# Two reciprocals per attention chunk, written as GpSimd powers with exponent minus one

## What is computed

```
fk = jnp.fft.rfft(k, axis=-1)
fk = fk / (jnp.abs(fk) + EPS)          # EPS = 1e-8
fq = jnp.fft.rfft(q, axis=-1)
fq = fq / (jnp.abs(fq) + EPS)
fv = jnp.fft.rfft(v, axis=-1)
fkv = jnp.cumsum(fk * fv, axis=-2)
values_hat = jnp.fft.irfft(fkv * jnp.conj(fq), n=D, axis=-1)
return x + values_hat
```

## Time and profile before

| | |
|---|---|
| median of three runs | 2069.51 us |
| lowest and highest run | 2063.09 and 2073.0 us |
| span of the profiled execution | 2101.2 us |
| attention stage, about | 750 to 1340 us of the span |
| VectorE busy in that stretch | 483.00 of 590 us |
| TensorE busy in that stretch | 395.29 of 590 us |
| GpSimd busy in that stretch | 175.54 of 590 us |
| ScalarE busy in that stretch | 154.13 of 590 us |

### The profile page before, as it was taken

How to read it: one execution, slowest core, us unless ns; L and a number is a source line. 1 busy time by engine, 2 the same in 40 slices (tenths; PEclk the granted TensorE clock), 3 DMA queues, 4 the chain that set the end, 5 groups by cost and what they waited for, 6 DMA issues and landing times.

```text
span 2101.2 us, 35984 instructions
## 1 busy us (share of the span) xinstructions
PE 1652.2 (79%) x10302; PEld 1458.4 (69%) x10303; DVE 1419.4 (68%) x3362; ACT 656.2 (31%) x1094; POOL 767.4 (37%) x868
## 2 busy tenths in 40 slices
PE   3999999679999647676767775599999967999940
PEld 2788888669999536555555553478888857999940
DVE  4778787535555368979898987377877753555557
ACT  3333333134444223232322231233333313444410
POOL 0454443324444323333333332144444422444420
PEclk9999999889999867776777776599999978999975
DMA  8211111144444311010101000011111114444459
GB/s 275 76 52 41 51 51 44 44 122 131 134 134 129 102 41 41 20 40 20 40 20 40 20 20 0 31 55 50 44 54 47 45 46 122 133 132 136 129 183 349
DMA packets 123782, 170.37 MB, mean 81 GB/s; under 512 B 14881, under 2 KB 105394, under 8 KB 123442
## 3 DMA queue, kind: packets, MB, share of 16 engines
q1 hardware_dynamic: 89938, 91.05, 15.0%
q0 software_dynamic: 25344, 70.29, 9.1%
q10 hardware_dynamic: 8448, 8.39, 1.1%
HBM read 91.03 MB, written 81.89 MB: 82 GB/s over the span
## 4 chain that ended last, share of the span: by engine, by line
PE 58%; DVE 17%; issue 9%; DMA 7%; ACT 3%; POOL 3%; SPq 2%; another core or an unknown queue 0%; DVEq 0%; POOLq 0%; ACTq 0%
PE bank L608 17%; PE bank L610 16%; PE bank L609 15%; PE bank L723 3%; DMA lists<-a_rows,a_slots 3%; POOL lists L405 3%; PE bank L733 2%; DMA f_yf<-results 2%; DVE t_cum L1151 2%; DVE t_rn L1133 2%; DVE a_gate_u L971 1%; PE bank L827 1%; DVE X L1214 1%; PE bank L632 1%; DVE t_pr L1149 1%
## 5 line engine op out<-in xcount | busy, mean ns | idle before, releaser
L416 POOL DMA_INDIRECT results<-b_yb,b_goal x272 | 261.6, 962 | 370.5 <-DVE b_yb L1074 297.8
L405 POOL DMA_INDIRECT lists<-a_rows,a_slots x256 | 259.7, 1014 | 117.5 <-issue 64.5
L1074 DVE COPY b_yb<-bank 128x512 f32<-128x512 f32 x136 | 94.1, 692 | 188.4 <-PE bank L610 180.0
L608 PE MATMUL bank<-t_xah,t_wfh 128*128 128x512 f32 x192 | 114.0, 594 | 111.8 <-DVE t_xal L848 61.7
L608 PE MATMUL bank<-ew_h,b_hth 128*128 x544 | 161.5, 297 | 20.3 <-issue 9.9
L608 PE MATMUL bank<-ew_h,b_xbth 128*128 x544 | 165.3, 304 | 1.0 <-DVE b_xbtl L848 1.0
L608 PE MATMUL bank<-a_sw2h,a_uh 128*128 128x256 f32 x512 | 150.4, 294 | 12.6 <-DVE a_ul L848 7.3
L455 ACT ACTIVATE b_hth<-bank 128x512 fp32r<-128x512 f32 x136 | 81.3, 598 | 246.7 <-PE bank L723 239.5
L609 PE MATMUL bank<-ew_l,b_xbth 128*128 x544 | 152.8, 281 | 0.0
L610 PE MATMUL bank<-ew_h,b_xbtl 128*128 x544 | 152.4, 280 | 0.0
L610 PE MATMUL bank<-ew_h,b_htl 128*128 x544 | 152.3, 280 | 0.0
(11 more groups left out here) (209 smaller groups left out, 5114.0 us busy)
## 6 DMA issues: line engine op xcount, KB each, us to landing
b_xb<-lists SPq DMA_DIRECT2D x272, 132.0 KB
t_yg<-results SPq DMA_DIRECT2D x32, 512.0 KB, 4.7
f_yf<-results SPq DMA_DIRECT2D x32, 512.0 KB, 10.9
X<-in_L_attn_x SPq DMA_DIRECT2D x16, 512.0 KB
out<-X ACTq DMA_DIRECT2D x16, 512.0 KB, 7.1
results<-b_yb,b_goal POOLq DMA_INDIRECT x272
w_raw_ew<-in_L_ffn_ew SPq DMA_DIRECT2D x2, 2048.0 KB, 14.3
lists<-a_rows,a_slots POOLq DMA_INDIRECT x256
```

Source lines behind the costliest of these rows:

```text
L405: pool.indirect_dma_start(out=lists, out_offset=bass.IndirectOffsetOnAxis(ap=slots[:, q, k, j:j + 1], axis=0), in_=rows[:, q, j, :], in_of ...
L416: pool.indirect_dma_start(out=results, out_offset=bass.IndirectOffsetOnAxis(ap=goal[:, slot, blk:blk + 1], axis=0), in_=YB[:, slot, blk, : ...
L608: pe.matmul(o, a("h"), b("h"), start=first, stop=False)
L1074: dve.tensor_copy(YB[:, slot].rearrange("p b d -> p (b d)"), bank[:, 7 - par, :]).then_inc(s_yok, 1)
```

## The change

The two reciprocals leave VectorE. Each becomes a GpSimd `tensor_tensor` with the operation power, whose second operand is the constant -1 of `neg_one`, read 512 times from one element per partition. VectorE keeps the two additions of the epsilon, which now signal `s_keps` and `s_qeps`; the multiplication of `FK` is moved behind the second of them and waits for `s_kinv`. On GpSimd the key power stands ahead of the addition to `X`, the query power behind it, followed by a wait for itself and the multiplication of `FQ`.

```diff
-DVE_A, DVE_T = 84, 57
+DVE_A, DVE_T = 84, 51
...
+            def inverse(i):
+                return pool.tensor_tensor(RN[:, i, :], RN[:, i, :], neg_one[:, 0:1].to_broadcast([P, N]), ALU.pow)
+
             def attention(s, par, half):
...
                 if nxt:
                     rstd_of(1 - par, s + (CH + 2))
+                if now:
+                    pool.wait_ge(s_keps, s + 1)
+                    inverse(0).then_inc(s_kinv, 1)
+                if nxt:
                     pool.wait_ge(s_txn, s + 2)
                     xc = X[:, bass.ds((s + 1) * J, J), :]
                     pool.tensor_tensor(xc, xc, XN[:], ALU.add).then_inc(s_add, 1)
                 if now:
-                    pool.wait_ge(s_qinv, s + 1)
+                    pool.wait_ge(s_qeps, s + 1)
+                    ch.link(inverse(1))
+                    ch.settle()
                     pool.tensor_tensor(FQ[:], FQ[:], RN[:, 1:2, :].to_broadcast([P, 2, N]), ALU.mult).then_inc(s_qn, 1)
...
-            run_steps(pool, attention, -1, 2, CH - 2, CH, 2, ch, 6)
+            run_steps(pool, attention, -1, 2, CH - 2, CH, 2, ch, 8)
...
                     dve.wait_ge(s_kroot, s + 1)
-                    ch.link(dve.tensor_scalar(RN[:, 0, :], RN[:, 0, :], FFT_EPS, None, ALU.add))
-                    ch.settle()
-                    ch.link(dve.reciprocal(RN[:, 0, :], RN[:, 0, :]))
-                    ch.settle()
-                    ch.link(dve.tensor_tensor(FK[:], FK[:], bc(RN[:, 0:1, :], [P, 2, N]), ALU.mult))
-                    if par == 1:
-                        ch.link(dve.tensor_copy(ny[:, 48:50], CUM[:, :, N - 1]))
-                    ch.settle()
+                    dve.tensor_scalar(RN[:, 0, :], RN[:, 0, :], FFT_EPS, None, ALU.add).then_inc(s_keps, 1)
                 if nxt:
                     dve.wait_ge(s_ah, s + 2)
                     low(XA["l"][:], bank[:, 0:2, :], XA["h"][:]).then_inc(s_al, 1)
                 if now:
                     dve.wait_ge(s_qroot, s + 1)
-                    ch.link(dve.tensor_scalar(RN[:, 1, :], RN[:, 1, :], FFT_EPS, None, ALU.add))
-                    ch.settle()
-                    dve.reciprocal(RN[:, 1, :], RN[:, 1, :]).then_inc(s_qinv, 1)
-
+                    dve.tensor_scalar(RN[:, 1, :], RN[:, 1, :], FFT_EPS, None, ALU.add).then_inc(s_qeps, 1)
+
+                    dve.wait_ge(s_kinv, s + 1)
+                    ch.link(dve.tensor_tensor(FK[:], FK[:], bc(RN[:, 0:1, :], [P, 2, N]), ALU.mult))
+                    if par == 1:
+                        ch.link(dve.tensor_copy(ny[:, 48:50], CUM[:, :, N - 1]))
+                    ch.settle()
                     dve.wait_ge(s_vps, s + 1)
```

More of the change, by code:

```diff
@@ L276, in build @@
                                                   sem("nyq_h"), sem("nyq_l"))
-        s_qinv, s_qn, s_ps, s_aps, s_aout = sem("q_inverse"), sem("q_norm"), sem("ps_ok"), sem("a_ps"), sem("a_out")
+        s_keps, s_qeps, s_kinv, s_qn, s_ps, s_aps, s_aout = sem("k_eps"), sem("q_eps"), sem("k_inverse"), sem("q_norm"), sem("ps_ok"), sem("a_ps"), sem("a_out")
         s_f = [sem(f"f_in{i}") for i in range(4)]
```

## The result

The changed kernel takes 4541.33 us in the median of four runs (4539.53 to 4544.28), the kernel before 2067.66 us (2063.09 to 2073.0, one more run than ahead of the prediction). The ratio is 2.196 with a 95% interval of 2.192 to 2.201. The forecast was 5340 us, with the direction slower; the range of 2005 to 5600 us holds the measured time, as does the likeliest case's own range of 4500 to 5600, near its lower end. The forecast itself is 799 us too high.

The account below looks back on a forecast made before the run. VectorE, with both reciprocals on the path, then TensorE's queue bound the attention chunk; two 106 us powers add 204 us a chunk, 3267 over 16, to 2101 us: 5368, less 31.7 for profiling, forecast 5340 us, range 2005 to 5600.

Parts of the forecast that it names:

- likeliest case's own range: Price paid by column, chance 0.55: 4500 us (a quarter of the excess paid per instruction) to 5600 us.
- What bounds the kernel: Attention stage: VectorE sets the pace up to t = 14.5 us, then TensorE's queue; both reciprocals, 6.7 us, lie on the path.
- The added powers on the path: Two GpSimd powers per chunk on 128x512: the key power holds the key product, the query power the FQ product.
- The price p: Time of one GpSimd power on 128x512, extrapolated from 128x4 rows: bounds 1.27 to 106 us, 106 taken.
- All 0.82 us are paid by the four columns: Upper bound for the 128x4 power's excess over a multiplication: 0.205 us a column, so 106 us on 512 columns.
- Who holds whom: Long GpSimd instructions, the 512-column power included, hold back VectorE's operations with both inputs in SBUF, and its epsilons.
- four columns may have been read long before: Caveat on a VectorE scan that ran in 0.22 us inside a 1.05 us GpSimd power on 128x4.
- The sum: Attention chunk, p a power's time: TensorE released at 2p + 6.7 us instead of 14.5, break-even p = 3.9 us.
- the term that I left at nothing: TensorE's 12 query spectrum matmuls all staying at the low clock after idling: 2.4 us a chunk, 40 us in all.
- Faster: Rival, chance 0.20: the power's excess is a start cost once per instruction; 2011 us, or 1962 if GpSimd holds nothing.
- Partly once, partly by column: Rival, chance 0.21: the power's excess is split; half and half gives 54 us, 3675 us; the case spans 2080 to 4500.
- The rule of about twice VectorE's time: Trainium skill's rule for elementwise GpSimd work: would put the power at the lower bound, 1.27 us; taken as denied.

Follow-up runs that it names:

- e9_arsqrt: From the kernel before: ScalarE's Abs_reciprocal_sqrt replaces Sqrt, and VectorE's epsilons and reciprocals of RN are left out; 1984.96 us, ratio 0.946.
- e2_widths: From the changed kernel: key power on 256 columns and query power on 64, the other columns not inverted; 2775 us.
- e3_even: From the changed kernel: both powers on 24 of the 512 columns only, the others not inverted; 2079.91 us, ratio 0.992.
- e6_query: From the kernel before: only the query inverse becomes a GpSimd power on 512 columns, the key's stays VectorE's reciprocal; 3348.24 us.
- e1_mult: From the changed kernel: the two GpSimd powers replaced by multiplications of the same operands and shape, output not normalized; 2041.3 us, ratio 0.974.

## Why the prediction was right, and where it missed

- **What bounds the kernel.** Right: both reciprocals lay on the path. e9_arsqrt, which removes them and the epsilons (7.6 us a chunk), brings the chunk from 34.9 to 27.5 us.
- **The added powers on the path.** Right: each one counts in full, 1215 and 1247 us alone, 2474 together, and the readers that the prediction named wait for them.
- **The price p.** The step that failed is "All 0.82 us are paid by the four columns". p is 82.4 us, not 106. Of the 0.82 us of excess at four columns, the runs give 0.157 to each column, 0.63 together, and leave 0.19 for the start. Divided by four and multiplied by 512, 0.19 us became 24 us a power, 47 us a chunk and 755 of the 799 us by which the forecast missed. The range's lower end, a quarter of the excess paid per instruction (80 us, 4500), was nearly the case that came. That the measured time is inside the likeliest case's own range hangs on 2 us in 80, and that is luck: nothing in the rows had set the border there.
- **Who holds whom.** Half right. GpSimd's additions and multiplications hold VectorE's operations with two inputs in SBUF, as the earlier trace rows had it; the power does not hold the scans, as the earlier trace rows had it, and I gave those rows too little weight. All sixteen first scans ran beside a power of 82 us in 1.22 to 1.29 us:

```profile
L1156 DVE TENSOR_TENSOR_SCAN t_cum<-t_pr x8: 1223/1224/1224, 840.6 to 3495.5; 128x512 f32<-128x512 f32 x8
L1156 DVE TENSOR_TENSOR_SCAN t_cum<-t_pr,t_ny x8: 1284/1284/1286, 1031.0 to 3683.9; 128x512 f32<-128x512 f32 x8
```

  The Trainium skill ("SBUF — State Buffer", section "Who interferes with whom") has the pair held for the whole instruction; for the power the measurement says otherwise. It does hold VectorE at its beginning, where no scan falls. In the last chunk, which has no addition to `X`, the `FK` product starts with the query power and takes 2.06 us, 0.83 more than its 1.23. And the copy of 128x2 that follows the `FK` product in every second chunk takes 1.00 us, against 0.16 in the kernel before:

```profile
3680.49 2.06 DVE L1149 TENSOR_TENSOR t_fk<-t_fk,t_rn 128x1024 f32<-128x1024 f32 x1 [81.82 <-POOL t_rn L428]
L1151 DVE COPY t_ny<-t_cum x8: 156/998/999, 1028.7 to 3682.5; 128x2 f32<-128x2 f32 x8
```

  Beside powers of 64 and 24 columns the same copy takes 0.25 and 0.18 us (e2_widths, e3_even), so this hold grows with the columns, by 1.0 to 1.6 ns each. The prediction's remark that four columns may have been read long before fits this: a power that reads its columns first and computes afterwards would look so, but no run shows what it does inside. In the other direction the `FK` product held back the power's start by 1.0 us (81.93 and 82.91 us in the two rows of one chunk; in e6_query, where no `FK` product meets it, the query power takes 81.94).
- **The sum.** The prediction had TensorE released at 2p + 6.7 and the query products at 2p + 9. In the chunk above, with t = 0 at 1132.98 us and p = 82.4, the `FK` product ends at p + 3.0, TensorE is released at 1222.2, which is p + 6.8 and far ahead of its turn, and the query products start at 1302.68, t = 169.7 or 2p + 4.9. The path runs through these products alone. From them to the next key epsilon's end it takes 20.0 us. In the chunk of the earlier trace rows this was 17.2, but that chunk is a short one (33.0 us): over fifteen chunks the mean is 19.9 us now and was 19.0 before, from 16.9 to 22.5. The back transform after an idle time of 78 us runs at the low level (1.2 GHz of 2.4; the granted clock of the stretch is 0.53, against 0.71 before), starting a matmul of 256 columns every 0.21 us, and takes 9.3 us from its first matmul to its last, where the chunk of the earlier trace rows has one every 0.12 us and 5.3 us in all:

```profile
1310.60 0.58 PE L617 MATMUL bank<-t_wih,t_vhh 128*128 128x256 f32 x1 [77.77 <-DVE t_vhl L857]
1310.98 0.41 PE L618 MATMUL bank<-t_wil,t_vhh 128*128 128x256 f32 x1
1311.19 0.41 PE L619 MATMUL bank<-t_wih,t_vhl 128*128 128x256 f32 x1
...
1319.46 0.41 PE L837 MATMUL bank<-t_sign,t_pnl 1*128 1x256 f32 x1
```

  The same stretch before, in the chunk of the earlier trace rows:

```profile
865.58 0.28 PE L609 MATMUL bank<-t_wil,t_vhh 128*128 128x256 f32 x1
...
870.49 0.28 PE L828 MATMUL bank<-t_sign,t_pnl 1*128 1x256 f32 x1
```

  Against these 4.0 us stand the 1.3 us by which TensorE came late to the low part before and does not now, and chunks of the kernel before that had a slow back transform too. So the term that I left at nothing (40 us) is there with some 16 x 1.0 = 16 us, in the back transform and not in the query spectrum.

  Together 2p + 24.9 = 189.7 us with p = 82.4. The prediction's steps with the measured p give 34.9 + 2 x 78.5 = 191.9, or 2p + 27.1. Apart from the price the sum is thus 2.2 us a chunk too high, 35 us of the kernel, and that is the holding that did not happen: it put TensorE's release behind the second power. One figure of the range was added up wrongly: its upper end of 5600 us comes to some 5520 by its own terms. Nothing hangs on it.
- **The rivals.** "Faster" fell with the price. Its mechanism is real where the operation is cheap: e1_mult gains 57 us with the same move, and e3_even still 18 at 4.2 us, or 4.6 with the overlap. The rule of about twice VectorE's time ("GPSIMD Engine Reference" of the Trainium skill, section 4.1) does not reach the power: 82 us stand against 3.35 of VectorE's reciprocal, 25 times. "Partly once, partly by column" is right in kind, with 0.19 of 0.82 us paid once; I had set its border at 80 us, 2 us below what came.

## What to carry to other kernels

A row at a tiny size gives the sum of a fixed part and a part per column, and a factor of 128 between that size and yours magnifies whatever is put on the wrong side: measure the operation at a second size before moving it, since two sizes give the line. Before work goes to an idle engine, compare its price with the break-even on the path, here 5 us a power against 82; idle time says nothing of price. When work leaves a bounding engine, look what it had covered: here a wait for ScalarE took about half of what a cheap operation had freed. And where a value is computed in two steps on two engines (root, then reciprocal), look for one operation that gives both on the engine that has time: that took 5.4% off here, with the two epsilons left out.

## What the runs showed of the hardware

- A GpSimd power on fp32 costs about 0.35 us and 0.159 us a column of 128 partitions, whether the exponent is -1 or -0.5. An addition costs 2.1 ns a column, so the power is some 75 times dearer by the column.
- A power on 512 columns holds VectorE for about its first 0.8 us (the `FK` product of the last chunk 2.06 us against 1.23, the 128x2 copy 1.00 against 0.16) and leaves it alone for the other 81, while a GpSimd addition of 2.34 us holds VectorE's operations with two inputs in SBUF until it ends: the `FK` product was stretched from 1.23 to 3.35 us in the median of the sixteen chunks. An operation with one input can be held too: the epsilon on 128x512 took up to 2.07 us against 0.42 beside that addition in e3_even. The runs do not show why the power behaves otherwise.
- ScalarE's Abs_reciprocal_sqrt on 128x512 takes 0.63 us like Sqrt, beside Copy, Square and Identity with no table loading between them but the one ahead of the first.
